# Attention over a graph, 8192 rows: the denominators of whole-row visits two pairs later, and another order at the end

## The reference

```
h = jnp.maximum(_layernorm(x, axis=-1), 0.0)          # x is 8192 x 256
h1 = h @ a[:d]; h2 = h @ a[d:]
e = jax.nn.leaky_relu(h1 + h2.T, negative_slope=0.01)
attention = jnp.where(adj > 0, e, NEG_BIG)
attention = jax.nn.softmax(attention, axis=1)
x = x + attention @ h
```

## Time and profile before

| | |
|---|---|
| Three runs | 1649.08, 1650.54, 2972.68 us |
| Profiled execution | 1649.05 us, its span 1647.3 us |
| TensorE matmul busy | 1602.7 us (97%), 13350 instructions |
| VectorE busy | 1431.8 us (87%) |
| ScalarE busy | 1182.4 us (72%) |
| GpSimd busy | 396.1 us (24%) |
| Mean granted TensorE clock | 0.997 |

### The profile page before, as it was taken

The page is one execution under the profiler, slowest core; times in us unless marked ns, Lnnn a source line. Parts: engine busy times, 40 slices in busy tenths (PEclk is TensorE's granted clock), DMA queues, the critical chain, the costliest instruction groups (busy, mean ns, idle before and its releaser), DMA issues.

```text
span 1647.3 us, 38960 instructions
## 1 busy us (share of the span) xinstructions
PE 1602.7 (97%) x13350; PEld 1591.9 (97%) x13350; DVE 1431.8 (87%) x2008; ACT 1182.4 (72%) x1240; POOL 396.1 (24%) x487
## 2 busy tenths in 40 slices
PE   4999999999999999999999999999999999999998
PEld 4899999999999999999999999999999999999998
DVE  6899999999999988888888888888888888888887
ACT  6788887777787776767767767767766766767763
POOL 4353233533454410201201201301300300400400
PEclk9999999999999999999999999999999999999999
DMA  5666768777778777656656765765756666666662
GB/s 168 200 214 218 223 189 251 228 233 244 237 216 251 223 214 235 197 174 192 209 173 188 213 183 174 227 174 182 214 176 195 205 182 181 205 184 190 205 181 75
DMA packets 170232, 330.45 MB, mean 201 GB/s; under 512 B 8624, under 2 KB 26032, under 8 KB 170160
## 3 DMA queue, kind: packets, MB, share of 16 engines
q1 hardware_dynamic: 145104, 288.38, 58.2%
q10 hardware_dynamic: 25056, 41.13, 7.5%
HBM read 308.38 MB, written 21.10 MB: 200 GB/s over the span
## 4 chain that ended last, share of the span: by engine, by line
PE 79%; issue 4%; DVE 4%; POOL 4%; ACT 3%; DMA 1%; ACTq 0%; DVEq 0%; POOLq 0%
PE acc L817 25%; PE acc L820 24%; PE acc L819 24%; PE T L779 6%; POOL stage L358 2%; DVE w_lo L669 1%; DVE W L659 1%; DMA xo<-part_sums 1%; POOL xb L369 1%; POOL xb L367 1%; ACT mask L462 1%; ACT hb L526 1%; ACT w_hi L471 1%; ACT stage L525 1%; ACT stage L490 0%
## 5 line engine op out<-in xcount | busy, mean ns | idle before, releaser
L817 PE MATMUL acc<-h_hi,w_hi 128*128 128x258 f32 (+1 forms) x4096 | 1184.5, 289 | 11.5 <-DVE w_lo L669 11.4
L820 PE MATMUL acc<-h_hi,w_lo 128*128 128x258 f32 (+1 forms) x4096 | 1155.4, 282 | 0.0
L819 PE MATMUL acc<-h_lo,w_hi 128*128 128x256 f32 (+1 forms) x4096 | 1150.1, 281 | 0.0
L471 ACT ACTIVATE w_hi<-W 128x1024 fp32r<-128x1024 f32 x512 | 538.4, 1057 | 360.0 <-DVE W L659 305.6
L817 PEld LDWEIGHTS acc<-h_hi,w_hi 128*128 128x128 f32 x4096 | 773.1, 189 | 16.0 <-ACT w_hi L471 14.3
L659 DVE SCALAR_TENSOR_TENSOR W<-r_rep,g_all,T 128x512 f32<-128x512 f32 (+1 forms) x1024 | 717.9, 742 | 70.4 <-DVE w_lo L669 41.2
L819 PEld LDWEIGHTS acc<-h_lo,w_hi 128*128 128x128 f32 x4096 | 778.1, 190 | 0.2
L820 PEld LDWEIGHTS acc<-h_hi,w_lo 128*128 128x128 f32 x4096 | 773.7, 189 | 0.0
L669 DVE SCALAR_TENSOR_TENSOR w_lo<-W,w_hi 128x1024 fp32r<-128x1024 f32 x512 | 652.3, 1274 | 104.7 <-PE acc L820 76.4
L462 ACT ACTIVATE mask<-adj_in,mhalf 128x2048 fp8e5<-128x2048 int32 x256 | 509.5, 1990 | 26.5 <-POOL xb L369 26.5
L367 POOL TENSOR_TENSOR xb<-xb,stage 128x256 f32<-128x256 f32 x60 | 55.7, 929 | 697.0 <-ACT hb L526 697.0
(11 more groups left out here) (63 smaller groups left out, 220.1 us busy)
## 6 DMA issues: line engine op xcount, KB each, us to landing
adj_in<-in_adj_dram SPq DMA_DIRECT2D x256, 1024.0 KB, 5.4
part_sums<-stage ACTq DMA_DIRECT2D x24, 516.0 KB, 6.9
xo<-part_sums ACTq DMA_DIRECT2D x24, 516.0 KB, 3.6
r_rep<-r_rows SPq DMA_DIRECT2D x39, 256.0 KB, 3.7
xb<-in_x_dram ACTq DMA_DIRECT2D x15, 512.0 KB, 3.8
out_dram<-xb ACTq DMA_DIRECT2D x15, 512.0 KB, 3.3
xb<-in_x_dram SPq DMA_DIRECT2D x14, 512.0 KB, 5.5
xo<-in_x_dram SPq DMA_DIRECT2D x2, 512.0 KB, 6.8
```

Of the source, the lines that this page charges most:

```text
L471: nc.scalar.activation(w_hi[:, k % HL, :], W[:, k % 2, :], ACT.Relu).then_inc(s_hi, 1)
L817: nc.tensor.matmul(acc[:, t, 0:WC], w_hi[:, k % HL, cols], rhs_hi, start=start and u == 0, stop=False)
L819: nc.tensor.matmul(acc[:, t, 0:D], w_hi[:, k % HL, cols], rhs_lo, start=False, stop=False)
L820: last = nc.tensor.matmul(acc[:, t, 0:WC], w_lo[:, k % LL, cols], rhs_hi, start=False, stop=stop and u == 1)
```

## The change

Two parts, and they share no code.

**In whole-row visits** `denominators` stands in slot 5 of VectorE in place of slot 3. `normalise` stands in slots 6 and 7 of ScalarE, two row tiles in each, in place of one in each of the slots 3 to 6. `store_out` stands in the first slot of the visit's last step (`2 * PI`), in place of slot 7. Quarter visits with `prev="full"` stay as they were.

**At the end** TensorE works off the last two pairs row tile by row tile: both pairs' share of tiles 0 and 1 pair by pair, then both for tile 2, then both for tile 3. VectorE's final operations for a tile are five: `zrow` and `den` come straight from the two denominator columns, `den` by a maximum with 1e-37 in place of adding `zrow`; `reciprocal` waits for `den` alone.

```
-    TAIL = 6
+    TAIL = 5
+    TINY = 1e-37
...
-                if V.prev in ("full", "rest"):
-                    if k == 2:
-                        load_x_again(V)
+                if V.prev in ("full", "rest") and k == 2:
+                    load_x_again(V)
+                if V.prev == "full":
                     if 3 <= k < 3 + G:
                         normalise(V.f, k - 3)
                     if k == 7:
+                        store_out(V)
+                if V.prev == "rest":
+                    if k in (6, 7):
+                        normalise(V.f, 2 * (k - 6))
+                        normalise(V.f, 2 * (k - 6) + 1)
+                    if k == 2 * PI:
                         store_out(V)
...
                     if second:
                         side_work(V, PI + k)
+                    if last and V.prev == "rest":
+                        side_work(V, 2 * PI + k)
...
-                if V.prev in ("full", "rest") and k == 3:
+                if (V.prev, k) in (("full", 3), ("rest", 5)):
                     denominators(V)
...
-                nc.vector.tensor_scalar(dsum[:, col], acc[:, t, D:D + 1], acc[:, t, D + 1:WC], None,
-                                        ALU.add).then_inc(s_tail, 1)
+                d_hi, d_lo = acc[:, t, D:D + 1], acc[:, t, D + 1:WC]
+                nc.vector.tensor_scalar(zrow[:, col], d_hi, d_lo, 0.0, ALU.add, ALU.is_equal).then_inc(s_tail, 1)
+                nc.vector.tensor_scalar(den[:, col], d_hi, d_lo, TINY, ALU.add, ALU.max).then_inc(s_tail, 1)
                 dve.wait_ge(s_tail, TAIL * t + 1)
-                nc.vector.tensor_scalar(zrow[:, col], dsum[:, col], 0.0, None, ALU.is_equal).then_inc(s_tail, 1)
-                dve.wait_ge(s_tail, TAIL * t + 2)
-                nc.vector.tensor_tensor(den[:, col], zrow[:, col], dsum[:, col], ALU.add).then_inc(s_tail, 1)
                 nc.vector.scalar_tensor_tensor(x_last[:, t, :], hmean, zrow[:, col], x_last[:, t, :],
                                                ALU.mult, ALU.add).then_inc(s_tail, 1)
+                dve.wait_ge(s_tail, TAIL * t + 2)
+                nc.vector.reciprocal(rinv[:, col], den[:, col]).then_inc(s_tail, 1)
                 dve.wait_ge(s_tail, TAIL * t + 4)
-                nc.vector.reciprocal(rinv[:, col], den[:, col]).then_inc(s_tail, 1)
-                dve.wait_ge(s_tail, TAIL * t + 5)
...
+            def last_products(c, g, k):
+
+                pe.wait_ge(s_hi, g + 1)
+                pe.wait_ge(s_lo, g + 1)
+                for t in range(2):
+                    row_tile(c, k, t, False, False)
+                pe.wait_ge(s_hi, g + 2)
+                pe.wait_ge(s_lo, g + 2)
+                for t in range(2):
+                    row_tile(c, k + 1, t, False, True).then_inc(s_acc, 1)
+                row_tile(c, k, 2, False, False)
+                row_tile(c, k + 1, 2, False, True).then_inc(s_acc, 1)
+                row_tile(c, k, 3, False, False).then_inc(s_used, 1)
+                row_tile(c, k + 1, 3, False, True).then_inc(s_used, 1)
...
+                    if V.tail and last and kc == 1:
+                        if k == 2:
+                            last_products(c + kc, n * PI + k, k)
+                        continue
```

## The result

The changed kernel takes **1678.06 us** (median of 4 runs, 1677.69 to 1678.96) against 1649.81 us for the kernel before in the same comparison: a ratio of **1.0175 (95% interval 1.0163 to 1.0187)**. It is 28 us slower. One of the four executions of the kernel before took 2972.68 us; the ratio leaves it out, and the median of the other three is 1649.08. 1654 was forecast, with a range from 1646 to 1668; the sign was right, the size wrong, and the time lies outside the range. The profiled execution took 1678.33 us, its span is 1676.5 us, its mean granted clock 0.983 (0.997 before).

What follows compares the result with a forecast made beforehand. TensorE, with matmuls in flight in 97% of the span, was taken as the bound; +6.8 in the visits and -2.8 at the end made +4.0 on 1649.05, 1653.1, stated as 1654 after the median; range 1646 to 1668.

Steps and rivals of the forecast that it cites:

- The pause before pair 2: Whole-row visits: TensorE's 1.39 us wait for w_lo goes, 8 x 1.39 = 11.1 us addressed; the moved denominators' 0.70 is free.
- The pause after pair 6: Whole-row visits: TensorE waits at least 2.5 us for ScalarE's mask; transposes 0.85 us later, +6.8 us over 8 visits.
- First normalise at 1051.5: ScalarE in a whole-row visit: the first normalise starts at 1051.5, behind rounding 6, and cannot be earlier.
- the rule for the two engines: Shared SBUF port: whichever of VectorE's two-SBUF-input operation or GpSimd's operation starts first keeps it; the other is blocked.
- GpSimd first, by 0.15: Tile 0 in a visit: GpSimd's second addition starts at 1053.3, before subtraction 6 is released at 1053.46 to 1053.5.
- the first link: Normalise plus GpSimd's two additions through single hshare: a tile costs the next one 0.89 + 1.68 = 2.57 us.
- The race of tile 1: Tile 1 in a visit: GpSimd's second addition ends about 1056.7, just ahead of subtraction 7's release at 1056.8.
- a rival at 1662: One GpSimd race lost in each visit: 8 x 1.85 - 2.8 = +12 us; shares 31 in 100 with the clock rival.
- The clock: Granted clock falls after each new pause: 0.5 to 0.7 us a visit, up to 1.7; +4 to +14 on top.
- races lost: GpSimd starts second in visits: one race a visit 1662, both 1670; 31 in 100 together with the clock falling.
- The last stretch: After the last subtraction: first final operation at 1637.13, 1.27 us a tile, in sum -2.8 us.
- the pause simply goes: Rival, whole-row visits: ScalarE's waits are hidden after all, 11.1 + 2.8 = 13.9 us gained, 1636; 14 in 100.

Runs made afterwards that it cites:

- the run that turned it: Changed kernel with three more VectorE operations in slot 7 of whole-row visits, so that GpSimd's addition starts first: 1667.49 us, ratio 1.0111.
- pauses of 2.77 us: Changed kernel with one normalise in each of slots 5 and 6 and two in slot 7: 1657.53 us, ratio 1.0049.

## Why the prediction was wrong

**The pause before pair 2** goes, and nothing else of the moved denominators costs anything: right. VectorE's 0.70 us are hidden.

**The pause after pair 6** as what the change turns the old one into: right in place, cause and sign. It was predicted at 2.5 us at least, with transposes 0.85 later in the visit than before; it is 3.75 us, and they are 1.70 later. Two steps were off. "First normalise at 1051.5", 13.22 us behind the release of subtraction 1, came at 13.59 (1063.31 - 1049.72): subtraction 2, which now runs while GpSimd adds the earlier sums (1050.10 to 1053.65), took 1.75 us in place of 1.22. Before the change VectorE stood idle there. The working had the rule for the two engines and applied it to one pair of operations and not to this one. Subtraction 3 then starts 6.45 us behind the release (1056.17), where the working had 6.16, and without idle time before it; so 0.29 of the 0.37 us stand there already, and the rest comes up to ScalarE's roundings. No run took that collision away alone, so that the delay comes from it is read from the trace, not shown. And "GpSimd first, by 0.15": the second addition of tile 0 starts 15.37 us behind the release, where the working had 15.02, and subtraction 6 at 15.08, where it had 15.18. The delay was more than the margin, the race of tile 0 was lost, and the first link took 3.41 us and not 2.57. (The race of tile 1 was won, 1068.43 against 1068.71.) That the lost race made the link long was shown by the run that turned it. The two errors, 0.37 and 0.84, are more than the 0.85 us that the transposes are late; the other two links came out 0.11 short of 2 x 2.57, and the rest was in the working's allowances. The prediction had this case as a rival at 1662; that value is right for what it describes: with work in the pause, and so without the fall of the clock, the kernel takes 1660.44.

**The clock** is what took the time out of the range: 17.5 of the 28.3 us. It was named as a rival and priced at 0.5 to 0.7 us a visit "by these counts" with 1.7 as the end; it costs 2.2. The step that failed is the comparison of 7 matmuls in a window at 0.50 with 1/0.119 = 8.4. A window's count has every instruction that overlaps it, and two or three matmuls are in flight at any time: at full clock it reads 11. So 7 is not five sixths of full speed but about half. The starts show it, 0.22 us apart at 0.50 and 0.12 at full clock:

```profile
1078.38 0.42 PE L821 MATMUL acc<-h_lo,w_hi 128*128 128x256 f32 x1
1078.60 0.42 PE L822 MATMUL acc<-h_hi,w_lo 128*128 128x258 f32 x1
...
1080.21 0.28 PE L821 MATMUL acc<-h_lo,w_hi 128*128 128x256 f32 x1
1080.33 0.28 PE L822 MATMUL acc<-h_hi,w_lo 128*128 128x258 f32 x1
```

The stretch was too short as well: "three or four such us", as behind 33.86, while seven of the eight visits work for some 5.3 us at half speed. The last error is the treatment as a rival beside "races lost". The price was put on top of the forecast, not on top of the lost race (1662 + 14 = 1676, which lies outside the range). With pauses of 2.77 us the clock stayed up in one execution, and the other three, with lower mean clocks, were 4 to 6 us longer; with 3.65 to 3.76 it fell in all eight visits. One mis-sized term moved a second mechanism over its edge, and the two were never added up.

**The last stretch**: -2.8 forecast, -2.8 measured; 1.27 a tile forecast, 1.26 measured. In the profiled execution the first tile's operations start 2.46 us behind the last subtraction's start (1669.33 - 1666.87), where 2.22 was worked out.

Put together: +4.0 forecast, +6.8 for transposes 0.85 us later than forecast in each of eight visits, +17.5 for the clock: 28.3.

The rival that ended as a gain ("the pause simply goes", 1636) was rightly given little for this kernel, but it was within reach: one normalise a slot, or three buffers, and the old pause goes with nothing in its place. TensorE wants the transposes 21.34 us behind the release of subtraction 1 (1059.62 - 1038.28); the first normalise starts at 13.59 and the conversion takes 2.1, so 5.6 us are left for normalises that need 9.25 with the single buffer and 4.23 with three.

## What to carry to other kernels

Work that is moved to make room on one engine must be followed on the engine that waits in order: two waits on another engine's answer directly behind each other cost two full round trips, where the same waits with other work between them cost TensorE nothing here (1629.52 us). When a step is made late, compute the arrival of whatever is queued behind it (here a conversion that had no slack at all), and where the result is a pause of some three microseconds on TensorE, add the price of its clock to it, not beside it. If the margin of a race between two engines is smaller than the error of the working, take the lost race for the forecast, or give the buffer one more copy and have no race.

## What the runs showed of the hardware that was not expected

- Behind a pause of 3.75 us on TensorE the granted clock is at 0.50, from inside the pause on, for 6.8 us, of which some 5.3 are work; a fall costs 2.2 us in the mean. In the first visit it fell only behind the pause and was down for 3.4 us. With pauses of 3.8 to 3.9 us (denominators back in slot 3) it was down for 3.4 us in five visits and for 6.8 us in three. Pauses of 1.4 us never did it. At 2.77 it was up all through one execution (mean 0.998), and the mean was lower in three others (0.994 to 0.996). With 3.02 to 3.15 it fell in seven of eight visits of one execution, and the transposes ran at either speed. 24 useless matmuls in the pause keep it up.
- VectorE's `w_lo` subtraction (two operands from SBUF) and GpSimd's additions hold each other up from both sides: an addition that starts second takes up to 1.60 us in place of 0.74, a subtraction that starts second up to 1.75 to 1.78 in place of 1.22. Work put on VectorE made a kernel faster because it changed who starts first.
